# Performer's query walk in pairs of tiles, with the output bias added in the key walk

## The reference

```python
def softmax_kernel_features(data, proj, is_query):
    data_dash = einsum('bhnd,md->bhnm', data_normalizer * data, proj)
    diag_data = sum(square(data), -1, keepdims=True) * 0.5 * data_normalizer**2
    stab = max(data_dash, -1) if is_query else max(data_dash)
    return ratio * (exp(data_dash - diag_data - stab) + EPS)
q1, k1 = features of q and of k
kv = einsum('bhnm,bhnd->bhmd', k1, v);  ksum = sum(k1, axis=2)
z = 1.0 / einsum('bhnm,bhm->bhn', q1, ksum)
out = einsum('bhnm,bhmd->bhnd', q1, kv) * z[..., None]
h = h + out.reshape(B, N, C) @ W_proj + b_proj
```

## Time and profile before

| | |
|---|---|
| median of 3 runs | 4424.52 us (4421.49 to 4429.08) |
| profiled execution | 4428.94 us, span 4427.1 us |
| busy over the span | PE 96%, PEld 74%, DVE 58%, ACT 49%, POOL 38% |
| granted TensorE clock, mean | 0.99 |
| key walk | 62 to 373 us of the span |
| query walk | 373 to 739 us of the span |

### The profile page before, as it was taken

How to read it: one execution, slowest core, us unless ns; L and a number is a source line. 1 busy time by engine, 2 the same in 40 slices (tenths; PEclk the granted TensorE clock), 3 DMA queues, 4 the chain that set the end, 5 groups by cost and what they waited for, 6 DMA issues and landing times. The chain is left out here.

```text
span 4427.1 us, 198366 instructions
## 1 busy us (share of the span) xinstructions
PE 4229.7 (96%) x86686; PEld 3276.6 (74%) x86686; DVE 2558.4 (58%) x7442; ACT 2190.1 (49%) x5035; POOL 1672.6 (38%) x2778
## 2 busy tenths in 40 slices
PE   6999999999979999999999999999999999999998
PEld 4666666677657777777777777777777787999998
DVE  5666887766645555665565556556665654432333
ACT  3443443555545555555555556555555553213444
POOL 1102334677653333333333333333333332002555
PEclk8999998999999999999999999999999999999999
DMA  4112110000000000000000000000000001332333
GB/s 112 24 24 55 40 40 7 1 2 1 1 14 4 15 5 16 23 12 8 16 15 6 13 16 16 4 16 16 16 4 16 16 15 35 79 87 60 65 64 56
DMA packets 122697, 114.40 MB, mean 26 GB/s; under 512 B 63974, under 2 KB 110395, under 8 KB 121843
## 3 DMA queue, kind: packets, MB, share of 16 engines
q1 hardware_dynamic: 94447, 66.34, 6.4%
q0 software_dynamic: 16768, 23.59, 3.0%
q10 hardware_dynamic: 10628, 11.80, 1.1%
HBM read 59.76 MB, written 41.48 MB: 23 GB/s over the span
## 5 line engine op out<-in xcount | busy, mean ns | idle before, releaser
L2246 PE MATMUL PS<-th_kT,th_qg 64*64 64x274 f32 (+1 forms) x21120 | 1446.5, 393 | 9.7 <-issue 8.6
L1941 POOL TENSOR_TENSOR th_qg<-th_qT,w_th_th 128x180 f32<-128x180 f32 x1760 | 851.4, 506 | 1364.1 <-PE PS L2246 1354.2
L2137 ACT ACTIVATE th_P<-PS 119x600 f32<-119x600 f32 x880 | 649.7, 738 | 850.6 <-PE PS L2232 850.3
L2246 PEld LDWEIGHTS PS<-th_kT,th_qg 64*64 64x64 f32 (+1 forms) x21120 | 841.1, 132 | 225.3 <-issue 35.2
L2055 DVE TENSOR_REDUCE th_nmx<-PS 125x1 f32<-125x548 f32 x880 | 640.4, 728 | 632.5 <-PE PS L2246 631.5
L2232 PEld LDWEIGHTS PS<-th_mixn,th_P 61*55 61x55 f32 x35200 | 661.7, 125 | 194.8 <-issue 81.2
L2232 PE MATMUL PS<-th_mixn,th_P 61*55 61x60 f32 x35200 | 696.9, 214 | 56.0 <-issue 49.6
L2147 ACT ACTIVATE th_P<-PS,th_nb 125x548 f32<-125x548 f32 x880 | 623.0, 708 | 109.0 <-DVE th_nb L2058 108.8
L1374 POOL TENSOR_SCALAR ga_P<-ga_P,ga_rw 110x110 f32<-110x110 f32 (+4 forms) x240 | 265.4, 1117 | 158.8 <-DVE ga_rw L1542 158.0
L2058 DVE TENSOR_SCALAR th_nb<-th_nmx,w_th_b 125x1 f32<-125x1 f32 x880 | 240.2, 273 | 32.2
L2271 PE MATMUL PS<-th_P,th_v 119*32 119x90 f32 (+1 forms) x11520 | 253.5, 244 | 4.3 <-issue 3.1
(11 more groups left out here) (366 smaller groups left out, 6412.7 us busy)
## 6 DMA issues: line engine op xcount, KB each, us to landing
pf_xT<-pf_spill SPq DMA_DIRECT2D x32, 412.5 KB, 5.4
ex_tokens<-th_xn SPq DMA_DIRECT2D x124, 82.5 KB
pf_spill<-pf_xT SPq DMA_DIRECT2D x16, 412.5 KB, 3.8
ex_turned<-th_rT SPq DMA_DIRECT2D x16, 412.5 KB, 3.1
ex_x<-ex_turned SPq DMA_DIRECT2D x32, 206.2 KB, 4.0
out_h<-X SPq DMA_DIRECT2D x16, 330.0 KB
ex_w<-in_L_ffn_W ACTq DMA_DIRECT2D x18, 288.0 KB
ex_w<-in_L_ffn_W ACTq DMA_DIRECT2D x8, 576.0 KB
```

The lines of the kernel that those rows point to most:

```text
L1941: ins = pool.tensor_tensor(qg[:, m % SB, :, 64 * s:64 * s + HQ].rearrange("p c (h n) -> p c h n", n=QH), qT[:, im % 2, :, at + s * QH:at + ...
L2137: act.activation(P2[:, :, :, at * QT:(at + 1) * QT].rearrange("p t h (s n) -> p s (t h) n", s=2), PS[0:PK, MB:MB + 2, 0:VO].rearrange("p s ...
L2246: ins = pe.matmul(PS[o:w, bank + a, 0:HK], qg[s, p, c, o:w], kT[s, im % 2, c, :], start=c == 0, stop=c == NC - 1)
```

## The change

The query walk's later half works on pairs of tiles. `numerators(p)` takes both tiles of a pair: eight heads of both tiles go to bank 6 (numerators, then denominators), the last four heads of both tiles to bank 7 (`RB`), 128 rows numerators and 128 rows denominators. So VectorE inverts once for 220 columns and once for 110, and multiplies likewise. `project(p)` takes the last four heads of the two tiles as two products of 64 rows, on different halves of the array, and then the two products of 128 rows; it writes banks 0 and 1, which the even tile's queries use as well, after the even tile's subtraction. VectorE adds both tiles' results to `X` in one instruction of 384 columns, and the next even `queries` waits for that. The bias is no longer a row of the weights: Pool adds it to `X` in the key walk, once an image, after the image's all-reduce.

```diff
                 sp.dma_start(pf.wp[:, 0, :], A["L0_attn_W_proj"][0:128]).then_inc(pf_in, 16)
-                sp.dma_start(pf.wp[0:D - 128, 1, :], A["L0_attn_W_proj"][128:D]).then_inc(pf_in, 16)
-                sp.dma_start(pf.wp[D - 128:D - 127, 1, :], row(A["L0_attn_b_proj"])).then_inc(pf_in, 16)
+                for a in range(2):
+                    sp.dma_start(pf.wp[a * PC:(a + 1) * PC, 1, :], A["L0_attn_W_proj"][128:D]).then_inc(pf_in, 16)
+                sp.dma_start(pf.bp[:], row(A["L0_attn_b_proj"]).broadcast_to([R, D])).then_inc(pf_in, 16)
...
-        z = sb("z", [128, 2, R])
-        oT = sb("oT", [128, 2, 2, R])
+        z = wz[:].rearrange("p b t h -> p (b t h)")[:, 0:3 * R]
+        oT = sb("oT", [128, 2, 3, R])
...
                         pool.partition_all_reduce(stab[:, b - 2:b - 1], top[:, b - 2:b - 1], 128, bass.bass_isa.ReduceOp.max) \
                             .then_inc(stabbed, 1)
+                        pool.wait_ge(xn_in, T * (b - 1))
+                        of = X[:, T * (b - 2):T * (b - 1), :]
+                        pool.tensor_tensor(of, of, bp[:].unsqueeze(1).broadcast_to([R, T, D]), ALU.add).then_inc(biased, 1)
...
+                def invert(p):
+                    if 0 <= p < STEPS:
+                        dve.wait_ge(num, p + 1)
+                        dve.reciprocal(z[:, 0:2 * R], PS[:, NB, 2 * R:4 * R])
+
+                def divide(p):
+                    if 0 <= p < STEPS:
+                        dve.reciprocal(z[:, 2 * R:3 * R], PS[:, RB, R:2 * R]).then_inc(recip, 1)
+                        dve.wait_ge(recip, p + 1)
+                        if p >= 2:
+                            dve.wait_ge(yprod, p - 1)
+                        dve.tensor_tensor(oT[:, p % 2, 0:2, :].rearrange("p i n -> p (i n)"), PS[:, NB, 0:2 * R], z[:, 0:2 * R], ALU.mult)
+                        dve.tensor_tensor(oT[:, p % 2, 2, :], PS[:, RB, 0:R], z[:, 2 * R:3 * R], ALU.mult).then_inc(oT_in, 1)
+
+                def add(p):
+                    if 0 <= p < STEPS:
+                        if p == 0:
+                            dve.wait_ge(biased, B)
+                        dve.wait_ge(yprod, p + 1)
+                        of = X[:, 2 * p:2 * p + 2, :]
+                        dve.tensor_tensor(of, PS[0:R, QB0:QB0 + 2, 0:D], of, ALU.add).then_inc(xadd, 1)
...
                         if u >= 2:
-                            act.wait_ge(num, u - 1)
+                            act.wait_ge(num, u // 2)
...
+                    if u % 2 == 0 and u >= 8:
+                        pe.wait_ge(xadd, u // 2 - 3)
...
+                def project(p):
+                    if 0 <= p < STEPS:
+                        pe.wait_ge(oT_in, p + 1)
+                        if p < STEPS - 3:
+                            pe.wait_ge(qsub, 2 * (p + 3) + 1)
+                        else:
+                            pe.wait_ge(xadd, p)
+                        for i in range(2):
+                            half = slice(i * PC, (i + 1) * PC)
+                            pe.matmul(PS[0:R, QB0 + i, 0:D], oT[half, p % 2, 2, :], wp[half, 1, :], start=True, stop=False)
+                        for i in range(2):
+                            ins = pe.matmul(PS[0:R, QB0 + i, 0:D], oT[:, p % 2, i, :], wp[:, 0, :], start=False, stop=True)
+                        ins.then_inc(yprod, 1)
```

More of the change, by code:

```diff
@@ L176, in early_weights @@
     pf.wp = sb(pf_ctx, "pf_wp", [128, 2, D])
+    pf.bp = sb(pf_ctx, "pf_bp", [R, D])
     pf.own34 = sb(pf_ctx, "pf_own34", [2 * M, 2 * (HD + 1)])
@@ L313, in _ @@
                 sp.wait_ge(text_in, 16 * (T + 1))
-                sp.wait_ge(pf_in, 16 * 7)
+                sp.wait_ge(pf_in, 16 * 8)
             @block.scalar
@@ L592, in performer @@
         gmax = sb("gmax", [128, 1])
-        w = sb("w", [R, B, T, H])
+        wz = sb("w", [128, B, T, H])
+        w = wz[0:R]
         e = sb("e", [R, RING, PAIRS, PW])
@@ L627, in performer @@
         oT_in, yprod, xadd = (sem(n) for n in ("oT_in", "yprod", "xadd"))
+        biased = sem("biased")
         STEPS = NT // 2
@@ L815, in _ @@
                 norm(1)
-                dve.wait_ge(filled, 4)
+                dve.wait_ge(filled, 3)
                 for s in range(KSTEPS):
@@ L876, in differ @@
                                       .broadcast_to([R, 2, HC, M]), ALU.subtract).then_inc(qsub, 1)
[L878 to L898, removed]
+                def invert(p):
[17 more added lines that the diff above has]
+                        dve.tensor_tensor(of, PS[0:R, QB0:QB0 + 2, 0:D], of, ALU.add).then_inc(xadd, 1)
+                for s in range(STEPS + 3):
                     a, b = 2 * s, 2 * s + 1
@@ L901, in _ @@
                         features(a)
-                    invert(b - 4)
-                    if a < NT:
                         differ(a)
-                    divide(b - 4)
-                    add(a - 4)
+                    invert(s - 2)
                     if a < NT:
                         features(b)
-                    invert(a - 2)
+                    add(s - 3)
                     if a < NT:
                         differ(b)
-                    divide(a - 2)
-                    add(b - 4)
+                    divide(s - 2)
             @block.scalar
@@ L991, in features @@
                                        bias=eps[0:2 * M, :]).then_inc(fT_in, 1)
-                for s in range(STEPS + 2):
+                for s in range(STEPS + 1):
                     a, b = 2 * s, 2 * s + 1
@@ L1081, in turn_features @@
                         ins.then_inc(fturn, 1)
[L1083 to L1092, removed]
-                                             start=True, stop=True)
[L1095 to L1102, removed]
-                        ins.then_inc(num, 1)
@@ L1105, in project, with numerators, column @@
[L1105 to L1111, removed]
+                def numerators(p):
+                    if 0 <= p < STEPS:
+                        pe.wait_ge(fT_in, 2 * p + 2)
+                        pe.wait_ge(kvmade, (2 * p + 1) // T + 1)
+                        if p >= 1:
+                            pe.wait_ge(oT_in, p)
+                        def column(w, i, j, g, bank, at):
+                            u = 2 * p + i
+                            return pe.matmul(PS[32 * g:32 * g + 32, bank, at:at + R], w[:, u // T % 2, j * 32:(j + 1) * 32], fT[:, u % 2, j, :],
+                                             start=True, stop=True)
+                        for i in range(2):
+                            for w, at in ((kvn, i * R), (kvd, (2 + i) * R)):
+                                for j in range(4):
+                                    column(w, i, j, j, NB, at)
+                        for w, at in ((kvn, 0), (kvd, R)):
+                            for i in range(2):
+                                for j in range(2):
+                                    ins = column(w, i, 4 + j, 2 * i + j, RB, at)
+                        ins.then_inc(num, 1)
```

17 lines of the change are left out of this document (6 added, 11 removed).

## The result

| | before | after |
|---|---|---|
| median of the runs, us | 4423.01 (4 runs, 4419.38 to 4429.08) | 4397.18 (4 runs, 4391.23 to 4403.09) |
| ratio, 95% interval | | 0.994 [0.9922, 0.9958] |
| profiled execution, us (span) | 4428.94 (4427.1) | 4403.09 (4401.3) |

What follows compares the result with a forecast made beforehand. TensorE was taken to bound the key walk, TensorE and VectorE to be near their limit in the query walk. 4428.94 less 21 gives 4408 profiled, less 4.4 gives a median of 4403.5 us; range 4391 to 4421.

Steps and rivals of the forecast that it cites:

- The bank loop: Query walk: next even query product waits for the addition, which waits for the projection; 8.14 us, TensorE idling 0.14.
- VectorE's order: Query walk: VectorE's operations walked through one step, idle behind the even maximum, 0.1 to 0.2 us to spare.
- The step, 8.14 predicted: Query walk, two tiles: from 8.71 to 8.14 us, gaining 0.57 in each of 37 steps, 21.1 us.
- Rival A: Query walk: TensorE pieces following their like are shorter, loop 7.99, 4391 to 4398 us; chance 0.17.
- the first steps: Query walk's first three steps: bound by the chain through one tile, which the pairs leave alone.
- The key walk, 0 predicted, and at most 1 to 2 once: Key walk: sixteen Pool bias additions cost TensorE nothing while two waits stay hidden; at most 1 to 2 us once.
- a later end of the key walk: Sign that the prediction would be wrong: the key walk no longer ending at 373 us.
- the longer chain: Key walk, first images: Pool's power, switch, all-reduce, switch, addition; power and all-reduce come about 2 us late.
- lead of 1.9 over the turns: Key walk, early image: VectorE normalises by 109.1, turns come at 111.04; 1.9 us of cover for a late all-reduce.
- I take 0, since TensorE in this walk waits for VectorE nearly nowhere: Key walk: VectorE held up beside Pool's addition, 2.2 us an image; bounds 0 to 35 us, taken as 0.
- the 2 us allowed: Drain after the query walk: one more step but half as many waits; counted 0, with 2 us either way.
- The load: First stage: one more small bias load on SP's queue; nothing in the sum, at most 1.58 us in the range.

Runs made afterwards that it cites:

- e1: Changed kernel with the odd tile's feature turn put ahead of the projection; step 8.82, median 4444.18 us, 1.0043 of the kernel before.
- e4: Changed kernel with the reciprocal shared by the two tiles' last four heads cut into two of 64 rows; median 4436.76 us, 1.0017 of the kernel before.
- e2: Changed kernel with both half-height projection products on rows 0 to 63 of the array; step 8.25, median 4414.41 us, 0.9983 of the kernel before.
- e3: Changed kernel with the projection's full products ahead of the half-height ones; step 8.13, median 4411.69 us, 0.9957 of the kernel before.

## Why the prediction was right, and where it was not

**The bank loop and VectorE's order: right in place.** The wait is at the addition and nowhere else; e1 shows that this loop sets the step, e4 that VectorE's room is 0.18 in the mean and 0.28 where Pool leaves it alone (0.1 to 0.2 predicted), e2 that the halves overlap. Reciprocal of 220: 1.52 (1.57); multiplication of 220: 0.39 (0.37); addition of 384: 0.56 (0.554).

**The step, 8.14 predicted, 7.94 measured: two terms too large.** Products of a pair 1.27 (507.21 to 508.48) and not 1.41; query product to projection 1.90 and not 2.00. The projection ends 1.33 after its start (1.26 predicted); from there to the next query product 0.74 (0.77). -0.14 - 0.10 + 0.07 - 0.03 = -0.20. The step that failed is the price of a passage: each old price held a change from one kind of product to another, and e3 puts that at 0.14 in the mean of two (0.10 of it for the query product alone). The rows of before held a sign of it: a turn and a tile's products took 0.70 + 0.71 in one half and 1.30 in the other, where the turn passes straight to a product of its own height; the sum counted 1.41 for both. Rival A had said so (7.99, 4391 to 4398), with 0.17 of the chance. For TensorE it was the better account, and the median, 4397.18, lies in its band and not in the forecast's own, 4398 to 4410. The gain is 37 x 0.776 = 28.7 and not 21.1. Between the profiles without a fallen clock the query walk is 30.2 shorter, 1.5 of it in the first steps, which the prediction took as unchanged.

**The key walk, 0 predicted, and at most 1 to 2 once: it costs 2.1** (mean 306.97 before, 309.1 after). By the prediction's own sign, "a later end of the key walk", it was wrong here. Two places in the first profile lose time, and both had been named. The first is the second image, VectorE behind the all-reduce (the earlier trace rows has 107.67 and 1.99):

```profile
111.08 0.28 DVE L826 SCALAR_TENSOR_TENSOR pf_w<-pf_diag,pf_stab,pf_low 110x60 f32<-110x60 f32 x1 [4.11 <-POOL pf_stab L716]
...
114.34 0.85 PE L1040 MATMUL PS<-pf_v,pf_e 110*89 110x68 f32 x8 [0.31 <-DVE pf_v L796]
```

That is 3.41 later, of which 0.86 is the later start and 0.39 the first products of keys, longer at half clock (6.67 after 6.28): 2.2 from the longer chain, as worked out. It uses up the lead of 1.9 over the turns, which lose next to nothing; what waits is the weighted products behind them (114.34). TensorE loses 0.57 in all, within the bound. The shortest idle time of Pool ahead of its small power was 9.36 and not 9.8, which changes nothing in this. The step that failed is the other one, "I take 0, since TensorE in this walk waits for VectorE nearly nowhere". It concerns the weighting beside Pool's addition (rows of both, and of TensorE):

```profile
172.51 2.20 POOL L720 TENSOR_TENSOR X<-X,w_pf_bp 110x960 f32<-110x960 f32 x1 [7.13 <-issue]
172.54 2.40 DVE L796 TENSOR_TENSOR pf_v<-pf_v,pf_w 110x204 f32<-110x204 f32 x1
...
175.00 0.29 PE L1040 MATMUL PS<-pf_v,pf_e 108*89 108x68 f32 x1 [0.38 <-DVE pf_v L796]
```

The weighting, else 0.35, takes 2.40, until 0.23 behind the end of Pool's addition. The Trainium skill (SBUF — State Buffer, "Who interferes with whom") says that an instruction holds the shared ports for its whole length; these rows agree. Over the walk the weightings grew from 27.9 to 40.9 us. Of these 13, TensorE loses 0.60, 0.41 and 0.28 in three images; elsewhere the cover held. With the 0.57 that makes 1.86, and 2.25 with the 0.39 of the first keys; the two profiles differ by 2.22 (308.90 and 306.68). The 0.39 is no sign of the change: in the third profile of before the first keys are 0.72 longer than in its first. Pool's addition itself took 2.20 (2.2 predicted).

**Drain and load.** The drain is 20.0 and 23.4 after, 18.4 to 21.2 before: 2.0 longer by the means, the whole of the 2 us allowed. Most of the spread goes with the clock (granted 0.82 and 0.64 after; 0.93 and 0.65 in the shortest and longest before). At like clock it is still 2.1 longer (0.64 after, 0.65 before) or 0.5 (0.82 and 0.85); why stays open. The load is not to be seen.

Together, means of the profiles from the first instruction to the last addition: 736.7 before, 711.0 after, -25.7, as the medians (-25.8 and -25.1). Forecast were -21: the step gained 7.6 more, the first steps 1.5, key walk and drain gave 4 back. That two misses offset each other, so that the total came nearer to the forecast than the step did, is luck.

## What to carry to other kernels

Price a piece from its start to the next one's, and note which piece comes next: joining like pieces saves the passages as well, here 0.1 to 0.14 us each. When a buffer is reused so that a new loop arises, put the work that does not belong to it inside its wait: one turn of features on the wrong side of the projection cost more than the whole change gave. And an addition moved to an idle engine is free only where the operations that it holds up (here VectorE's weightings, 0.35 that became up to 2.40) have that much lead at every image.

## What was not expected of the hardware

The lower clock did not follow from the wait alone: the same wait of 2.29 us led to 1.2 GHz for 6.8 us (granted clock 0.5) in one profile and to nothing in five others; in the drain it falls sooner or later, and two profiles of one kernel lie 3 us apart there. What decides it no run here shows. A reciprocal's time goes by the elements of a row and not by the number of partitions: 110 elements took 0.83 on 64 and 0.83 on 128 partitions, 220 took 1.52.
